# Message passing: other durations in the plan that sets aggregation batches between gate products

## What is computed

```python
for i in range(STEPS):
    m = h @ W[i]
    msg = m[src] * emask[:, None]
    agg = jax.ops.segment_sum(msg, dst, num_segments=N)
    h = _gru_cell(agg, h, wih, whh, bih, bhh)
```

## Time and profile before

| what | us |
|---|---|
| median of 3 runs | 3041.75 |
| lowest and highest run | 3037.07 to 3042.34 |
| span of the profiled execution | 3036.4 |
| three message passing steps, first to last product | 614.3 to 1201.4, 1257.0 to 1841.9, 1898.7 to 2478.6 |
| PE busy | 2646.3 (87%) |
| DVE busy | 1592.0 (52%) |
| POOL busy | 1358.7 (45%) |

### The profile page before, as it was taken

One profiled execution on the slowest core, in us unless ns is written; L12 is line 12 of the kernel. 1 busy time (PEld: TensorE's weight loads), 2 busy tenths in 40 slices (PEclk: granted clock), 3 DMA queues, 4 the chain that ended last, 5 costly groups with the idle time before them and its releaser, 6 DMA issues. The chain is left out here.

```text
span 3036.4 us, 39301 instructions
## 1 busy us (share of the span) xinstructions
PE 2646.3 (87%) x13041; PEld 1701.2 (56%) x13041; DVE 1592.0 (52%) x3119; ACT 642.5 (21%) x1180; POOL 1358.7 (45%) x1375
## 2 busy tenths in 40 slices
PE   5898899779988898798899996898888966999997
PEld 3434455465555556554455554654545556788886
DVE  6798777445555554355555552466766784011110
ACT  3211000111111114111111123122212221332232
POOL 0000500066666661666666634666666600333333
PEclk7899999889999999899999998899999985999998
DMA  4300766334444443444444434343444423133223
GB/s 129 132 1 1 286 240 218 117 104 129 144 144 137 138 135 104 126 125 145 128 129 145 145 97 157 118 121 112 123 129 124 122 58 100 35 90 92 65 64 72
DMA packets 201473, 362.85 MB, mean 120 GB/s; under 512 B 27937, under 2 KB 156109, under 8 KB 201104
## 3 DMA queue, kind: packets, MB, share of 16 engines
q0 software_dynamic: 67776, 169.95, 20.2%
q1 hardware_dynamic: 129564, 186.48, 18.4%
q10 hardware_dynamic: 3956, 4.19, 0.5%
HBM read 293.37 MB, written 70.34 MB: 120 GB/s over the span
## 5 line engine op out<-in xcount | busy, mean ns | idle before, releaser
L1453 POOL DMA_INDIRECT xnT<-h_rows,idx x780 | 775.2, 994 | 378.0 <-issue 206.6
L1124 PEld LDWEIGHTS g_pagg<-g_onehot,xnT 128*128 128x128 f16 x4680 | 337.1, 99 | 408.3 <-issue 396.3
L1124 PE MATMUL g_pagg<-g_onehot,xnT 128*128 128x144 f16 x4680 | 416.0, 230 | 154.8 <-issue 152.8
L1295 DVE TENSOR_TENSOR g_agg<-g_agg,g_pagg 128x288 f32 x585 | 265.1, 453 | 370.6 <-remote 159.6
L1453 POOL DMA_INDIRECT xnT<-xn_rows,idx x366 | 360.6, 985 | 198.8 <-issue 95.0
L1298 DVE SCALAR_TENSOR_TENSOR g_onehot<-iota_keys,shift,keys 128x288 f16<-128x288 f16 x585 | 299.1, 513 | 0.6 <-DVE g_pre_at L1287 0.3
L1201 PE MATMUL g_pr<-g_agg,g_wc 128*128 128x448 f32 (+1 forms) x576 | 231.1, 520 | 18.1 <-DVE g_agg L1295 9.1
L1387 DVE SCALAR_TENSOR_TENSOR g_t<-g_ph,g_bh,g_rT 128x448 f32<-128x448 f32 (+1 forms) x144 | 89.8, 624 | 282.3 <-remote 199.1
L1201 PE MATMUL g_pz<-g_hT,g_wh 128*128 128x448 f32 (+1 forms) x576 | 224.4, 509 | 9.9 <-issue 5.9
L1201 PE MATMUL g_pz<-g_agg,g_wc 128*128 128x448 f32 (+1 forms) x576 | 228.8, 520 | 1.1 <-issue 0.9
L1201 PE MATMUL g_pr<-g_hT,g_wh 128*128 128x448 f32 (+1 forms) x576 | 224.8, 512 | 3.7 <-issue 3.5
(11 more groups left out here) (356 smaller groups left out, 3371.7 us busy)
## 6 DMA issues: line engine op xcount, KB each, us to landing
ma_R<-q_cols SPq DMA_DIRECT2D x27, 896.0 KB, 12.0
f_w<-in_L_ffn_W SPq DMA_DIRECT2D x16, 1024.0 KB, 7.7
h_cols<-g_hn SPq DMA_DIRECT2D x36, 448.0 KB
h_rows<-g_rows SPq DMA_DIRECT2D x36, 448.0 KB
g_hT<-h_cols SPq DMA_DIRECT2D x36, 448.0 KB
mix_R<-q_cols SPq DMA_DIRECT2D x15, 896.0 KB, 9.6
xnT<-h_rows,idx POOLq DMA_INDIRECT x780
ma_R<-q_cols SPq DMA_DIRECT2D x9, 1120.0 KB, 5.9
```

Of the source, the lines that this page charges most:

```text
L1124: mm = e.matmul(pg[:, k * TYPES:(k + 1) * TYPES, :].rearrange("p t d -> p (t d)"), rows[:, c, o:o + P], hot[:, c, :], start=(c == 0 and pa ...
L1295: e.tensor_tensor(agg[:, :, bass.ds(o, DT)], agg[:, :, bass.ds(o, DT)], pagg[b % BANKS][:, :, :], ALU.add).then_inc(S["added"], 1)
L1453: e.indirect_dma_start(ring[:, b % SLABS, c, :], None, tables[s], bass.IndirectOffsetOnAxis(ap=idx[:, o:o + 1], axis=0)).then_inc(landed[b ...
```

## The change

Four numbers of the planner are replaced: a batch lands every 2.61 us instead of 2.5, with 3.5 instead of 2.5 on top; a batch costs PE 0.5 instead of 0.56, a full product 1.54 instead of 1.56. No instruction is added or removed.

```diff
-LEAD, LANDS, ARRIVES, COUNTS, GATES, SLACK = 17.0, 2.5, 2.5, 0.56, 1.56, 8.0
+LEAD, LANDS, ARRIVES, COUNTS, GATES, SLACK = 17.0, 2.61, 3.5, 0.5, 1.54, 8.0
```

## The result

| | before | after |
|---|---|---|
| median us | 3039.41 (3033.43 to 3042.34, 4 runs) | 2989.94 (2985.75 to 2992.76, 4 runs) |
| ratio | | 0.9837, interval 0.9821 to 0.9854 |
| profiled execution, span | 3036.4 | 2986.3 |
| step 1, first to last product | 614.3 to 1201.4 | 616.3 to 1179.8 |
| step 2 | 1257.0 to 1841.9 | 1239.9 to 1803.2 |

The account below looks back on a forecast made before the run. PE, busy 87% of the span, was taken as the bound, with stalls that come with gathers. Terms 4.2 + 1.5 + 0.7 + 1.5 - 5 = +2.9 us per step, +9 for three, gave 3051 us (range 3020 to 3074).

Parts of the forecast that it names:

- Term 5: Groups 1 to 5 get thinner, and some stalls go with the batches: -5 us a step, bounds 0 and -16.
- term 3: Row of batches ahead of group 1 grows from 4 to 6, two more at 0.86: +0.7 us a step.
- terms 1: Twelve batches in a row ahead of group 7 run at DVE's pace, delaying its second product: +4.2 us a step.
- thinner groups dissolve the stalls: Rival for the message-passing groups: gathers get rest, stalls go, faster at 3013 or 3028 us; chance 0.25.
- Term 4: Gathers go on to the end of group 6, so stalls there last longer: +1.5 us a step, between 0 and 3.5.
- Term 2: PE's granted clock falls behind the row of twelve ahead of group 7: +1.5 us a step, between 0 and 3.

Follow-up runs that it names:

- e10: Changed planner with 2.7 us a landing and 2.5 for the first (groups of 25 to 26, row of 18): 2996.21 us, 0.9868 of the kernel before.
- e19: Changed kernel with one GpSimd memset behind each batch's two gathers: 3032.53 us, 0.9896 of the kernel before.
- e8: Kernel before with dummy VectorE reductions ahead of some reset gates in groups 1 to 6: 3094.61 us, 1.0197 of the kernel before.
- e6: Kernel before, word for word, on a chip with prompt signals: 2780.45 us, ratio 1.0007.
- e17: Kernel before with one of each batch's two gathers left out: 2748.50 us, 0.8975 of the kernel before.
- e18: Kernel before with as many gathers, each half as wide: 3063.86 us, 1.0007 of the kernel before.
- e20: Changed kernel with two GpSimd memsets behind each batch's gathers: 3055.19 us, 0.9977 of the kernel before.
- e16: Changed kernel without the steps' gathers, batches using rows already in the ring, on a late-signal chip: 2741.32 us.
- e5: Changed kernel, word for word, on a chip with prompt signals: 2782.85 us, 1.0016 of the kernel before.
- e15: Kernel before without the steps' gathers, batches using rows already in the ring, on a late-signal chip: 2731.50 us.
- e21: Changed kernel with e19's single memset and e10's plan: 3030.17 us, 0.9893 of the kernel before.

## Why the prediction was wrong

**Term 5 failed, by its size.** It put the stalls that go with thinner groups at 5 us a step, between 0 and 16. They are 29: groups 1 to 5 lose 36.3, 35.8 and 35.9 us in the three steps (the first from 416.6 to 380.3 us, by the traces' group bounds), less 6.5 for the batches themselves. Group 0 loses 5.0 in the mean, to which the prediction gave nothing beyond the +0.7 of term 3. By step, with 0.50 us for each batch moved taken out (us):

| part | forecast | step 1 | step 2 | step 3 |
|---|---|---|---|---|
| groups 1 to 5 (term 5) | -5 | -29.8 | -29.3 | -29.4 |
| group 0 with its row (term 3) | +0.7 | -8.7 | -3.8 | -2.5 |
| group 6, row, group 7 (terms 1, 2, 4) | +7.2 | +14.9 | +11.6 | +19.6 |
| the step | +2.9 | -23.6 | -21.6 | -12.3 |

The prediction treated a stall as something laid on top of a plain 72.9 us. In the runs with late signals a dense group (25 batches or more) is nearly a number of batches times a **pace** of 3 us, whatever its products cost:

| batches | groups in the mean | length, us | us a batch |
|---|---|---|---|
| 30 | after, group 6 without its row | 89.0 | 2.97 |
| 29 | before, groups 3 to 5 | 85.8 | 2.96 |
| 28 | before, group 2 | 83.4 | 2.98 |
| 27 | after, group 2 | 79.4 | 2.94 |
| 26 | after, groups 3 to 5 | 77.3 | 2.97 |
| 26 | e10, groups 2 and 5 | 74.4 | 2.86 |
| 26 | e19, groups 3 to 5 | 78.6 | 3.02 |
| 25 | e10, groups 3 and 4 | 75.1 | 3.00 |
| 24 | before, group 1 | 75.3 | 3.14 |
| 21 | after, group 1 | 68.8 | 3.28 |
| 29 | e8, with 15.4 us more on DVE | 86.1 | 2.97 |

Single groups scatter by some 4 us about these means (with 26 batches, after: 74.4 to 81.4), and group 1, whose first six products have no batch among them, takes more for each. So a batch taken out of groups 2 to 5 saves about 2.96 us, and at the end of the row, where POOL has done, it costs 0.86. The number stands in the prediction: "stalled groups already run at 86 / 29 = 2.96 us a batch, far above 2.52, and still stall". It was used as evidence against the rival. As a price it would have given 26 x 2.96 = 77.0 for groups 3 to 5, which the trace after shows as 77.3; the prediction's closing part had 84.5 without and 80.5 with the stalls gone. The 1.26 us per batch between 24 and 29 batches was drawn through group 1, which has that stretch without batches and so is no measure of what one costs.

**The rival "thinner groups dissolve the stalls" had the sign and too small a price**: 3013 to 3028. Its point of decision, whether POOL gets to rest, was not what decided. POOL waits for a slot as long after as before: beside the earlier trace rows there are 122.2 us "remote" before, 275.3 in all or 0.48 for each of 573 batches; after,

```profile
POOL xnT L1453 <- PE g_pagg L1124: 134.8, 77, 14.7
POOL xnT L1453 <- remote: 133.6, 88, 4.4
```

it is 268.4, or 0.47, and 2.52 + 0.48 is the pace of 3.0. In e6, with prompt signals, POOL waits 45.1 us. A loop fits all this: while POOL issues without rest PE's signals stay back; POOL rests only when the ring is full; the ring is freed only by PE's signal. It would give one pace for all dense groups, absorb e8's delays, vanish in e17, where POOL waits 794.6 us, and leave e18 as it was. e19 doesn't contradict it (0.15 us more a batch is less than the 0.48 taken anyway, and its pace is 3.02), and in e20 the 0.49 more are as much. That is a reading of these runs, not shown by one of its own. What in the chip holds PE's signals back, and why on some chips alone, was not found.

**Term 4 was too small.** Group 6 without its row takes 86.5 us for 30 batches in step 2, 13.0 above its plain 73.5, with POOL busy to its end. Before it was 8.2 above. That is +4.8, and in steps 1 and 3 it is +7.4 and +13.1; the prediction took +1.5, and its upper value of 3.5 was too low too. It expected the group at 83 to 87 us; the three are 89.1, 86.5 and 91.3, which is the same pace (2.97) as in the groups before. Step 2 is the step where terms 1, 2 and 4 came out best.

**Terms 1 and 2 held.** The row of twelve: expected 11.0 us from the first batch to the second product and an extra of 4.2; without gathers (e16) the stretch is 11.0, 10.6 and 11.0 us in the three steps, and the extra 4.0 to 5.2. With late signals it is 14.2, 13.4 and 12.5, so 2.3 more in the mean than 11.0; in step 2 DVE's adds at its beginning come late (the holes of 1.22 and 0.83 us). Term 2 had 1.5 for that. Its mechanism is only in part what was expected: the granted clock over the row is 0.86, 0.85 and 1.00, not 0.5. In e16 the row has the holes of DVE's pace alone, and the clock of its group 6 with the row is 1.00. Term 3's row of six adds 0.2 to 0.4 us without gathers; with late signals it is lost in the -5.0 of group 0, which no term foresaw.

**The code fetch.** The prediction read the late matmuls inside a batch as late code, and set the trace against the Trainium skill's "Runtime: NRT & Kernel Launch", section "Instruction fetch mechanics", which has fetching hidden. e5 is the changed kernel word for word, its code queues carry 95 and 82 packets as in the earlier trace rows, and PE is busy 71.00 of 71.00 us in the window shown. With that section's rule this trace agrees: fetching the same code does not stop PE by itself. Over the three steps the holes of more than 0.15 us inside a batch number 104 before (64.3 us) and 51 after (41.3), 1 in e17, and none in e5, e6, e15 and e20. So they go with the late signals, and the prediction was wrong to lean on them against the rule. What they are is open: no semaphore stands there, and no run shows whether code comes late while signals do.

**The step under all of them**: the stalls were taken for a property of the kernel, to be priced from rows of one execution. In three of the six sets of runs above they don't exist. There terms 1 and 3 alone, +4.9 a step or 14.7 in all, are near what the runs without gathers show (12.8 and 9.8 us); with gathers e5 stands 2.4 us above e6, since it saves waits for landings in the groups and pays for some in the row. For the forecast's own number this did not matter, as the trace that it was made from and the result both have late signals; it matters for what the change is worth elsewhere.

## What to carry to other kernels

Divide the length of a stalled stretch by each thing counted in it before splitting it into "plain" and "stall": where the quotient is the same for different counts, it is a pace, and each unit moved elsewhere is worth the whole of it, as long as the place it goes to is free of what sets the pace (in e10's longer row it was not, and a batch cost 3.0 us there too). A wait that ends "remote" while the producer had long ended is a late signal; add such waits up by engine before arguing about schedules. And time a plan on more than one chip: these durations are worth 1.6% on one kind and -0.1 to -0.2% on the other.

## What the runs showed of the hardware

- The same kernel takes 2778 to 2780 us on some chips and 3036 to 3062 on others. The lag of PE's semaphore updates is 0.01 us for at least nine in ten of them on the first kind and 1.9 to 2.2 us in the mean on the second; ACT's sigmoid starts 0.03 us behind the product on the first and 1.2 to 1.75 on the second.
- On the second kind the lag is there only while GpSimd issues indirect gathers (0.01 us in e15 and e16 and in group 7). It goes with their number or with the rest between them (two gathers a batch: 2.2 us; one: 0.13; two at 3.01 us a batch: 0.67) and not with their bytes (half as wide: 2.3). Between ACT and DVE there is none of it (0.04 us at most from DVE's candidate to the tanh).
- While signals are late, groups of 25 to 30 batches take 2.9 to 3.0 us a batch, though PE's work for such a group and POOL's for a batch would allow 72.9 us a group and 2.52 us a batch.
- The number of the chip does not tell the kind: the one named 3 gave 2779.3 us for the kernel before in e5 and e6, and 3061.6 in e19 to e21. Whether these were two chips of different machines or one that changed is open.
- In rows of batches PE keeps DVE's pace, 0.86 us a batch, where signals are prompt and data are there, and on the second kind once POOL has issued its last gather. While it still gathers, a row is slower (nine batches of e10's row in 22.1 us) and the granted clock falls: 0.88 over e10's group 6 with its row, against 1.00 in e16's.
